# Moving bulk loads, zero fills, a swap, a reduction and two value products within the opening of a gated cross-attention and routed-experts kernel

## The reference, cut to what matters

```
n = layernorm(x)                                   # over the 512 columns
q, k, v = Wq n + bq, Wk ctx + bk, Wv ctx + bv      # per batch (256, 512)
q, k = rotary(q), rotary(k)
prob = softmax(q k / 4)                            # 16 heads, 512 x 512
x = x + tanh(g_xattn) * (Wm (prob v) + bm)
m = layernorm(x)
x = x + tanh(g_ffn) * sum over 2 chosen experts of w_e * wo_e(silu(m w0_e) * (m w1_e))
```

## Time and profile before

| | |
|---|---|
| median of 3 runs | 1220.56 us (1219.19 to 1223.28) |
| profiled execution | 1225.02 us, its span 1223.2 us |
| TensorE (PE) busy | 1100.4 us, 90% of the span |
| VectorE (DVE) busy | 794.7 us, 65% |
| ScalarE (ACT) busy | 683.8 us, 56% |
| GpSimd (POOL) busy | 371.3 us, 30% |
| DMA | 153.09 MB, mean 125 GB/s |

### The profile page before, as it was taken

The page is one execution under the profiler, slowest core; times in us unless marked ns, Lnnn a source line. Parts: engine busy times, 40 slices in busy tenths (PEclk is TensorE's granted clock), DMA queues, the critical chain, the costliest instruction groups (busy, mean ns, idle before and its releaser), DMA issues.

```text
span 1223.2 us, 17330 instructions
## 1 busy us (share of the span) xinstructions
PE 1100.4 (90%) x5417; PEld 441.0 (36%) x5417; DVE 794.7 (65%) x1558; ACT 683.8 (56%) x932; POOL 371.3 (30%) x444
## 2 busy tenths in 40 slices
PE   3585999999999999997737999999999999999996
PEld 1121333333333333322223444444444444444442
DVE  6775877878687877877465465656646665564631
ACT  1263777777777777767605365655536564462521
POOL 3445364747373837312310111111111111101001
PEclk8787999999899999989668999999999999999999
DMA  6752332212131313132346566676747676564443
GB/s 227 231 176 88 132 133 89 84 63 99 54 105 56 112 44 132 53 106 87 108 172 165 112 175 171 157 189 148 192 74 203 139 203 141 134 197 76 68 57 58
DMA packets 189654, 153.09 MB, mean 125 GB/s; under 512 B 130176, under 2 KB 150656, under 8 KB 189568
## 3 DMA queue, kind: packets, MB, share of 16 engines
q1 hardware_dynamic: 176736, 127.15, 36.1%
q0 software_dynamic: 7744, 18.09, 8.1%
q10 hardware_dynamic: 5088, 6.79, 1.8%
HBM read 73.28 MB, written 41.75 MB: 94 GB/s over the span
## 4 chain that ended last, share of the span: by engine, by line
PE 74%; ACT 10%; issue 5%; DVE 4%; DMA 3%; POOL 1%; SPq 1%; ACTq 1%; POOLq 0%; DVEq 0%
PE psum L1156 31%; PE psum L1166 15%; PE psum L332 7%; ACT wh L466 7%; PE psum L319 6%; PE psum L217 4%; PE psum L259 3%; PE psum L307 3%; PE psum L227 2%; PE psum L277 1%; DVE MX L651 1%; ACT wh L423 1%; DMA scr<-wh 1%; ACT Xr L459 1%; PE psum L241 1%
## 5 line engine op out<-in xcount | busy, mean ns | idle before, releaser
L1156 PE MATMUL psum<-wh,xT 128*128 128x512 f16 x1728 | 380.6, 380 | 17.7 <-DVE xT L1238 17.6
L466 ACT ACTIVATE wh<-psum,es 128x512 f32<-128x512 f32 x512 | 320.7, 687 | 88.4 <-PE psum L319 84.4
L651 DVE TENSOR_REDUCE MX<-psum 128x2 f32<-128x1024 f32 x256 | 310.1, 1221 | 86.9 <-PE psum L307 85.7
L1156 PEld LDWEIGHTS psum<-wh,xT 128*128 128x128 f16 x1728 | 169.3, 98 | 223.2 <-issue 20.5
L1166 PE MATMUL psum<-wh,hT 128*128 128x512 f16 x864 | 194.1, 381 | 3.4 <-DMA hT<-hn 3.4
L319 PE MATMUL psum<-stg 50*128 50x512 f16 x512 | 151.2, 404 | 36.2 <-ACT wh L466 23.2
L1320 POOL DMA_INDIRECT out<-yb,target x36 | 56.2, 1561 | 337.6 <-ACT yb L1197 337.6
L1270 DVE TENSOR_TENSOR hh<-sg,psum 128x512 f32<-128x512 f32 x72 | 49.4, 686 | 157.0 <-ACT sg L1187 157.0
L332 PE MATMUL psum<-wh,vT 128*32 128x512 f32 x1024 | 146.4, 647 | 0.0
L531 ACT ACTIVATE wh<-stg,scw 128x1024 f16<-128x1024 f32 x96 | 103.0, 1138 | 49.7 <-DVE c L583 34.5
L538 DVE SCALAR_TENSOR_TENSOR wh<-stg,scw,wh 128x1024 f16<-128x1024 f32 x96 | 117.3, 1279 | 18.9 <-ACT wh L531 18.9
(11 more groups left out here) (197 smaller groups left out, 1014.9 us busy)
## 6 DMA issues: line engine op xcount, KB each, us to landing
stg<-in_w SPq DMA_DIRECT2D x16, 2048.0 KB, 10.3
stg<-in_wo SPq DMA_DIRECT2D x8, 2048.0 KB, 10.6
stg<-scr SPq DMA_DIRECT2D x186, 64.0 KB, 2.3
Xs<-zero SPq DMA_DIRECT2D x40, 264.0 KB, 2.8
wh<-wh SPq DMA_DIRECT2D x64, 128.0 KB, 2.0
scr<-wh SPq DMA_DIRECT2D x32, 256.0 KB, 2.3
out<-xs SPq DMA_DIRECT2D x8, 512.0 KB, 3.1
xs<-in_x SPq DMA_DIRECT2D x4, 512.0 KB, 6.6
```

What stands on the lines that cost most here:

```text
L466: act.activation(m.Pb[:, c % 2, hh, :], m.psT[tile % 2], ACT.Exp, scale=m.es[:, min(hb // 2, 2):min(hb // 2, 2) + 1]).then_inc(S["exped"], 1)
L651: dve.tensor_reduce(m.MX[:, hb % 2, c0:c0 + 9:8], m.psS[tile % 2], AX_X, ALU.max, negate=True).then_inc(S["maxed"], 1)
L1156: last = pe.matmul(m.psum[:, 2 * j + w, :], m.xT[:, 4 * xp + k, :], m.wh[(e % 2, w)][:, wp, c:c + 512], start=(k == 0 and xp == 0 and wp = ...
```

## The change

- TensorE: jobs v0 and v1 move from phase -2 to phase -1, steps 3 and 6, each cut in two halves, the second a step later.
- ScalarE: the read-outs of v0 and v1 move to phase -1 as well. After k1 and the second root it issues the context loads of batches 2 to 7 (before: x of 4 to 7 and context of 3 to 7, after v1).
- SyncE: context 2 and x 3 are no longer loaded at the start; x 3 to 7 are loaded after the stacks of half-batch 2, which themselves now stand in front of phase 0. swap(0, 3) stands behind max_rows(1). The fills start in phase 0 and run to phase 3, four blocks twice in each.
- GpSimd: far_largest stands between the two ropes of half-batch 3. far_roots stands in phase 2.
- VectorE: statistics of tiles 6 and 7 are taken in phase 1 with those of 8 to 15.

```diff
@@ jobs_at
     if ph == -2:
-        return [("q", 1), ("k", 1), ("v", 0), ("v", 1)] if s == 0 else []
+        return [("q", 1), ("k", 1)] if s == 0 else []
+    if ph == -1:
+        return {0: [("q", 2)], 3: [("v", 0)], 6: [("v", 1)], 9: [("m", 0)], 10: [("k", 2)]}.get(s, [])
@@ tensor_attention
-    def values(i):
+    def values(i, ccs=(0, 1)):
...
-        for cc in range(2):
+        for cc in ccs:
...
-        last.then_inc(S["valued"], 1)
+        if 1 in ccs:
+            last.then_inc(S["valued"], 1)
...
+                if ph == -1 and s in (4, 7):
+                    values(s // 7, ccs=(1,))
                 for kind, i in jobs_at(ph, s):
-                    if ph == -1 and kind in "qk":
+                    if ph == -1 and kind in "qkv":
                         turn((kind, i))
-                        project("qk".index(kind), i, its=(0,))
+                        if kind == "v":
+                            values(i, ccs=(0,))
+                        else:
+                            project("qk".index(kind), i, its=(0,))
@@ scalar_attention
     job("k", 1)
-    job("v", 0)
-    root(2, 2, 8)
-    job("v", 1)
-    for b in range(4, NB):
-        load_x(act, m, S, io, b)
-    for b in range(3, NB):
+    root(2, 2, 6)
+    for b in range(2, NB):
         load_ctx(act, m, S, io, b)
@@ vector_attention
-        for i in range(8, 16):
+        for i in range(6, 16):
             step.more(dve.bn_aggr(m.mv[:, i, :], m.bst[:, i, :]))
...
-        if ph == 1 and s < 8:
-            stats(8 + s, 9 + s)
+        if ph == 1 and s < 10:
+            stats(6 + s, 7 + s)
...
-    stats(2, 8)
-    variances(2, 8)
+    stats(2, 6)
+    variances(2, 6)
@@ pool_attention
-        if ph == 3:
+        if ph == 2:
             far_roots()
...
         for w in range(2):
+            if ph == 0 and w == 1:
+                far_largest()
             if ph + 3 < NH and (w, ph + 3) not in EARLY:
                 rope_steps(pool, step, m, S, w, ph + 3)
-        if ph == 0:
-            far_largest()
@@ sync_attention
     load_x(sp, m, S, io, 2)
-    load_ctx(sp, m, S, io, 2)
-    load_x(sp, m, S, io, 3)
     swap(0, 0)
...
     max_rows(1)
+    swap(0, 3)
     keep(1, 2)
-    fill_rows(0)
-    fill_rows(4)
+    stack(sp, m, S, 0, 2)
+    stack(sp, m, S, 1, 2)
+    for b in range(3, NB):
+        load_x(sp, m, S, io, b)
     for ph in range(0, LAST + 1):
         a = ph + 3
-        if ph + 2 < NH:
+        if 0 < ph and ph + 2 < NH:
             stack(sp, m, S, 0, ph + 2)
             stack(sp, m, S, 1, ph + 2)
...
-        if a < NH:
+        if 0 < ph and a < NH:
             swap(0, a)
...
-        if ph < 3:
-            fill_rows(8 * (ph + 1))
+        if ph < 4:
+            fill_rows(8 * ph)
...
-        if ph < 3:
-            fill_rows(8 * (ph + 1) + 4)
+        if ph < 4:
+            fill_rows(8 * ph + 4)
```

More of the change, by code:

```diff
@@ L145, in attention @@
         self.ve, self.y, self.yi, self.ya = sb("ve", [128, 2]), sb("y2", [128, 2]), sb("yi", [128, 2], I32), sb("ya", [128, 2])
-        self.vx, self.yxi, self.yxa = sb("vx", [128, 8]), sb("yxi", [128, 8], I32), sb("yxa", [128, 8])
+        self.vx, self.yxi, self.yxa = sb("vx", [128, 10]), sb("yxi", [128, 10], I32), sb("yxa", [128, 10])
         self.L, self.IX, self.IF = sb("L", [128, 2, 8]), sb("IX", [128, 2, 8], U32), sb("IF", [128, 2, 2])
@@ L639, in guesses @@
         step.settle()
-        for i in range(8, 16):
+        for i in range(6, 16):
             step.more(dve.bn_aggr(m.mv[:, i, :], m.bst[:, i, :]))
         step.settle()
-        step(dve.tensor_scalar(m.vx[:, :], m.mv[:, 8:16, 1], EPS, None, ALU.add))
+        step(dve.tensor_scalar(m.vx[:, :], m.mv[:, 6:16, 1], EPS, None, ALU.add))
         step(dve.tensor_scalar(m.yxi[:, :], m.vx[:, :].bitcast(I32), 1, None, ALU.arith_shift_right))
-        dve.tensor_scalar(m.rstd[:, 8:16].bitcast(I32), m.yxi[:, :], -1.0, float(0x5F3759DF), ALU.mult, ALU.add).then_inc(S["x_guess"], 1)
+        dve.tensor_scalar(m.rstd[:, 6:16].bitcast(I32), m.yxi[:, :], -1.0, float(0x5F3759DF), ALU.mult, ALU.add).then_inc(S["x_guess"], 1)
     def reduce_scores(hb, i):
@@ L876, in vector_attention @@
     rope_steps(dve, step, m, S, 1, 0)
-    stats(2, 8)
-    variances(2, 8)
+    stats(2, 6)
+    variances(2, 6)
     k_scale(1)
     dve.wait_ge(S["std"], 2)
-    dve.reciprocal(m.rstd[:, 2:8], m.rstd[:, 2:8]).then_inc(S["rstd_near"], 1)
+    dve.reciprocal(m.rstd[:, 2:6], m.rstd[:, 2:6]).then_inc(S["rstd_near"], 1)
     dve.wait_ge(S["rstd_near"], 1)
@@ L928, in far_roots @@
         pool.wait_ge(S["x_guess"], 1)
-        newton(pool, step, m.rstd[:, 8:16], m.yxa[:, :], m.vx[:, :]).then_inc(S["rstd_far"], 1)
+        newton(pool, step, m.rstd[:, 6:16], m.yxa[:, :], m.vx[:, :]).then_inc(S["rstd_far"], 1)
         pool.wait_ge(S["rstd_far"], 1)
```

## The result

The changed kernel is a little slower, where a gain of 11.6 us was forecast: 1225.97 us (median of 10 runs, 1224.40 to 1231.75) against 1221.47 us for the kernel before (10 runs, 1219.19 to 1225.38). The ratio is 1.0045, its 95% interval 1.0028 to 1.0061.

The account below looks back on a forecast made before the run. TensorE, 90% busy, was taken as bound by three early idle holes caused by SyncE's order and GpSimd's all-reduce. 3.0 + 4.5 + 9.0 + 1.8 - 5.2 - 1.5 = 11.6 us gave 1209.0, range 1202 to 1215.5.

Parts of the forecast that it names:

- Step 1: Before the first score: two loads fewer ahead of the first swap bring the first score 1.2 us earlier.
- Rival (b): Opening: context loads take the DMA engines from stack(1,0), keep(0,1) and keep(1,1); 5 us lost against forecast, 1214; chance 0.12.
- (c): Phase 1 start: x loads hold back max_rows(2), 2 to 4 us wait stays, q4 cold; 1212 to 1215; chance 0.11.
- (d): Phase 0, GpSimd: both code exchanges stretch beside x loads and fills; slower beyond 11.6 us of stretch; chance 0.04.
- Steps 2 and 3: Phase -1: values add 1.0 us and lower clock 1.6; max_rows(0) comes hidden; phase 0 at 58.7, 3.0 us won.
- Hole A: TensorE's idle time from 57.3 to 61.7, before phase 0, waiting for the row of maxima; forecast to be hidden.
- Step 4: Between phases 0 and 1: swap(0,3) behind max_rows(1) closes TensorE's idle time from 93.45 to 97.9; 4.5 us won.
- Step 5: Before q4: far_largest between ropes closes TensorE's idle time from 98.7 to 107.8; 9.0 us, plus 1.8 from clock.
- Step 6: At step 8 of phase 1: max_rows(3) lands late, a new wait of 5.2 us, plus 1.5 from lower clock.
- Step 7: Phases 1 to 3: later statistics, far_roots and fills cost 0; bounds 3.4 us for far_roots, 2.4 for fills.
- order part: Moves of swap(0,3) on SyncE and far_largest on GpSimd; 8.6 us of gain forecast.
- bulk part: Moves of bulk loads, fills, values and statistics; 3.0 us of gain forecast.

Follow-up runs that it names:

- e1_ctx_late: Changed kernel, with ScalarE issuing the six context loads only when the key stack of half-batch 0 has landed: 0.9978 of the kernel before.
- e5_both: Changed kernel with context loads waiting for stack(1,0), and swap(0,4) and max_rows(3) ahead of keep(1,3): 0.9926 of the kernel before.
- a2: The changed kernel, unaltered, profiled once more: 1226.5 us.
- e6_x_later: As e5_both, with the five x loads behind max_rows(2) instead of ahead of swap(1,3): 0.9890 of the kernel before.
- e2_order_alone: Kernel before, with only swap(0,3) moved behind max_rows(1) and far_largest between the ropes of half-batch 3: 0.9956 of the kernel before.
- e7_values_back: As e6_x_later, with v0 and v1 back in phase -2, ahead of the first score: 0.9921 of the kernel before.

## Why the prediction was wrong

At q5, up to which the steps reach, the forecast was 140.46 - 11.6 = 128.9 and the trace shows 139.5: 10.6 us missed, which the trace divides up.

- **Step 1, the first score at 35.3: measured 41.1, 5.8 us of the miss.** This is the step that failed. It bounded the delay of stack(1,0) by what that transfer gained (2.2 us). The loads' data in fact flowed from 30 us on (the DMA engines were 98% busy from 30 to 32), while only the first pieces of the stack had gone. The nearest rows were there: in the kernel before keep(1,1) had taken 9.9 us beside ScalarE's loads and the six pieces of stack(0,1), issued at 40.99, had taken 7.3 us (median). Step 3 even used the first, as a bound for keep(1,1) alone. Rival (b), at 0.12, named the mechanism and the place (first score at 40 to 41); its price of 5 us was near (5.7 at phase 0). The rivals were priced one at a time, though; the run had (b), the edge of (c) and half of (d) together. The Trainium skill (DMA: Bandwidth & Descriptors, section on queues, rings and completion order) has the engines take turns between queues packet by packet; from 32 to 34 us the turns gave q1 0.05 MB and q10 0.50 MB, so turns are no protection for the smaller transfer. e1_ctx_late showed the cause: with the loads held back the first score came at 34.07.
- **Steps 2 and 3.** From the first score to phase 0 the forecast had 23.4 us and the trace has 23.3. In e1_ctx_late, whose clock is lower at that point, it is 25.9, and in e5_both 22.4. Hole A closed as forecast.
- **Step 4, hole B closed: 1.98 us remain,** its upper bound (rival (c)). In a2 and e1_ctx_late this wait is gone. Phase 0 also took 0.6 us more. (The step's own sum, 20.2 + 10.8, is 31.0 and not 31.3; nothing hangs on it.)
- **Step 5, hole C closed: right,** even with an exchange of 10.6 us, since k_scale(2) asks late enough. The exchange's length was wrong: 5.8 forecast. Rival (d) named the stretch and was set aside because the old exchange ran beside four fills and took no longer. That row was read rightly and carried over wrongly: beside the four fills the exchange isn't longer, beside the x loads it is (e5_both and e6_x_later). Only one of the two exchanges fell beside them, so the break-even of (d), 11.6 us, was not reached: it cost 4 to 5.
- **Step 6, the new wait: 6.7 us against 5.2.** It was right for the mechanism and place; that the size comes near is in part luck. The row came 5.2 us later relative to phase 0 than forecast (57.6 instead of 52.4 us), nearly all of it the exchange, and TensorE wanted it 3.7 us later than forecast: phase 0 0.6, hole B 2.0, q4 at 2.91 instead of 1.98 us. Two misses nearly cancel: in e2_order_alone, with the exchange at 6.36 us, the row came almost when forecast and the wait was 0.85 us. The Trainium skill's 6 us for the first call (GPSIMD Engine Reference, section 2.1) is what the runs without x loads beside the exchange show, and too low by 4 to 5 us with them.
- **Step 7** put the fills of phase 3 at 0, with 2.4 us as the bound. It named the place: four of them stand ahead of max_rows(8), and TensorE now waits 0.85 us for that row at 205.16 (up to 1.64 us in the other traces with these fills). So it isn't nothing. The first scatter, at 210.43, also waits 1.70 us for fills; the scatter isn't on TensorE's path there. No wait of TensorE for statistics or far_roots was seen.

In sum: first score 5.8, phase 0 0.6, hole B 2.0, way to step 8 1.1, wait 1.5, and 0.4 back in phase -1 and behind the wait: 10.6 us. The sign of the order part was right and its size roughly: 8.6 us forecast (steps 4 to 6), 5.4 measured alone (e2_order_alone). Its terms fit less well than their sum: there the new wait was nearly absent, but phase 0 and the way to step 8 took 4.9 us more than forecast. The bulk part was forecast at 3.0 us of gain and measured at 11.4 of loss.

The miss is 17.0 us against the medians, though. Behind q5 the two traces differ by 0.3 us. The other 6.1 come from setting single executions against medians: the old page lay 4.5 us above its median, which the forecast took off as the same for both, and the new one lies 1.6 below its own. What the median lost, 4.5 us, is only in part in the opening (q5 at 138.9 on the mean of three executions before, at 140.1 on that of two after). In the stretch behind q5 executions differ by more without a cause that was found, and so where the other 3 us went stays open. The wait at phase 4, 1 to 1.6 us in most of these traces, is the one candidate that they show; no run has the late fills taken back alone.

## What to carry to other kernels

Before a bulk load is moved, list the small transfers that will be in flight beside it, on any queue, and price each by the worst landing that the trace shows beside bulk, not by how far it overlaps. When a reduction needs other code on GpSimd, moving it earlier moves two exchanges in front of whatever GpSimd does next; follow that work to the issuing engine and to everything queued behind its wait. Here one reordered pair of issues (swap(0,4) and max_rows(3) ahead of keep(1,3)) was worth at least as much as the whole order part (0.8% against 0.4%).

## What the runs showed of the hardware

- The last 64 KB piece of a stack on SyncE's queue landed 9 us after issue, and a 256 KB copy 10.6 us, beside six 512 KB loads on ScalarE's queue (the changed kernel); without such loads 1.8 to 2.8 us and 2.3 us (the kernel before). In 2 us the queues moved 0.05 and 0.50 MB.
- GpSimd's exchange of code took 5.8 to 6.4 us ahead of a partition all-reduce and 6.8 to 7.8 us behind it. Beside five 512 KB loads from device memory it took 10.5 to 11.4 us ahead and 10.6 and 11.3 us behind (e6_x_later, e7_values_back); beside four 264 KB fills to device memory 5.8 to 6.0 (the kernel before, e6_x_later).
- Executions of one program (the kernel before, three times) differed by up to 3.9 us in their first 140 us and by up to 6.7 us behind it.
- From its start to q4, waits taken off, phase 0 took 35.2 us where the granted clock fell to 0.50 from 69 to 77 us (e2_order_alone), and 32.6 us where it was 1.00 there (the kernel before).
